# Edge counts kept as running totals and subtracted on reload, and chunk maxima carried in bfloat16 parts, in a graph network

## What is computed

```python
def sage(x, Wl, bl, Wr):                       # twice
    agg = segment_sum(x[src], dst) / max(deg, 1)
    return relu(agg @ Wl + bl + x @ Wr)
# gru: messages = segment_sum(x[src] @ W + b + embed[edge_type], dst); x = gru_cell(messages, x)
# gin, three layers: agg = segment_sum(relu(h[src] + edge_attr_16 @ W), dst); a two-layer MLP follows
def gat(x, ea, Wl, bl, Wr, br, We, att):       # three layers, 4, 4 and 1 heads
    xl, xr = x @ Wl + bl, x @ Wr + br
    m = leaky(xl[src] + xr[dst] + ea @ We)
    s = (m * att).sum(-1)                      # one score per edge and head
    smax = segment_max(s, dst)
    ex = exp(s - smax[dst])
    return segment_sum(xl[src] * ex, dst) / segment_sum(ex, dst)
```

## Time and profile before

| | us |
|---|---|
| median of 3 runs | 11598.76 |
| lowest and highest | 11585.36, 12062.77 |
| the profiled execution | 11593.12 |
| its span, first to last instruction | 11591.3 |
| busy in the span: TensorE, VectorE, ScalarE, GpSimd | 7698.1, 5644.0, 3139.2, 4843.4 |
| counting stage, sage 1, gat stages | 120 to 1506, 1534 to 1764, 6233 to 11550 |

### The profile page before, as it was taken

The page is one execution under the profiler, slowest core; times in us unless marked ns, Lnnn a source line. Parts: engine busy times, 40 slices in busy tenths (PEclk is TensorE's granted clock), DMA queues, the critical chain, the costliest instruction groups (busy, mean ns, idle before and its releaser), DMA issues. The chain is left out here.

```text
span 11591.3 us, 187130 instructions
## 1 busy us (share of the span) xinstructions
PE 7698.1 (66%) x44683; PEld 5505.4 (47%) x44684; DVE 5644.0 (49%) x15775; ACT 3139.2 (27%) x10374; POOL 4843.4 (42%) x5412
## 2 busy tenths in 40 slices
PE   5998888644554444544546777776777776777776
PEld 2444478433343223322334555555555554555554
DVE  6888811222222222222224565666555666555556
ACT  1000130111111111101113444444444444333333
POOL 0011100365554665465653444443444443444442
PEclk9999999766676666666667777777777777777777
DMA  1000076222221111111111222221222221222221
GB/s 35 17 28 39 40 295 233 91 67 66 68 70 50 47 47 47 44 47 46 48 46 46 57 59 57 58 56 52 59 58 57 59 56 49 58 57 58 57 56 45
DMA packets 501818, 732.17 MB, mean 63 GB/s; under 512 B 128746, under 2 KB 406594, under 8 KB 485013
## 3 DMA queue, kind: packets, MB, share of 16 engines
q1 hardware_dynamic: 350484, 414.14, 10.8%
q0 software_dynamic: 150528, 308.58, 10.3%
HBM read 597.78 MB, written 124.32 MB: 62 GB/s over the span
## 5 line engine op out<-in xcount | busy, mean ns | idle before, releaser
L542 POOL DMA_INDIRECT rows_and_onehots<-node_table,idx x4704 | 4560.3, 969 | 2748.4 <-issue 1373.3
L802 PE MATMUL ps<-rows_and_onehots,w 128*128 128x128 f32 x5280 | 1010.7, 353 | 2010.6 <-ACT w L674 1464.1
L802 PEld LDWEIGHTS ps<-rows_and_onehots,w 128*128 128x128 f32 x5280 | 940.9, 260 | 2597.3 <-issue 2564.8
L674 ACT ACTIVATE w<-w 128x512 f32<-128x512 f32 x663 | 417.5, 630 | 3387.8 <-DVE w L1224 2776.9
L951 PE MATMUL ps<-w_L_gnn_We,hr 128*128 128x512 f32 x1344 | 1113.3, 923 | 174.6 <-issue 119.7
L537 POOL COPY idx<-src_g 128x8 int32 (+1 forms) x594 | 115.3, 194 | 2541.4 <-DVE hr L1407 1111.9
L1224 DVE TENSOR_TENSOR w<-rows_and_onehots,ps 128x512 f32<-128x512 f32 x663 | 456.2, 688 | 1272.3 <-issue 689.8
L962 PE MATMUL ps<-hr,rows_and_onehots 128*128 128x132 f32 (+1 forms) x5280 | 955.5, 335 | 116.3 <-DVE hr L1407 87.3
L954 PEld LDWEIGHTS ps<-xrb,w 128*128 128x128 bf16 x8064 | 715.8, 125 | 634.8 <-issue 634.8
L1353 DVE TENSOR_TENSOR w<-rows_and_onehots,ps 128x512 f32<-128x512 f32 x669 | 458.5, 685 | 1042.1 <-remote 817.5
L978 PE MATMUL ps<-ident,scanned 20*128 20x20 f32 (+1 forms) x1332 | 339.1, 330 | 928.9 <-DVE scanned L1359 791.5
(11 more groups left out here) (223 smaller groups left out, 11786.0 us busy)
## 6 DMA issues: line engine op xcount, KB each, us to landing
w<-turned_onehots_bf SPq DMA_DIRECT2D x672, 128.0 KB
rows_and_onehots<-node_table,idx POOLq DMA_INDIRECT x4704
hr<-in_ea SPq DMA_DIRECT2D x672, 64.0 KB
w<-adjacency_turned SPq DMA_DIRECT2D x26, 1600.0 KB, 7.0
adjacency<-rows_and_onehots SPq DMA_DIRECT2D x25, 1600.0 KB, 5.2
w<-adjacency SPq DMA_DIRECT2D x25, 1600.0 KB, 12.0
rows_and_onehots<-adjacency_turned SPq DMA_DIRECT2D x24, 1600.0 KB, 7.7
turned_onehots_bf<-w SPq DMA_DIRECT2D x224, 128.0 KB
```

The lines of the kernel that those rows point to most:

```text
L542: pool.indirect_dma_start(out=G[q][:, (i % CH) * D:(i % CH + 1) * D], out_offset=None, in_=table[:, :], in_offset=bass.IndirectOffsetOnAxi ...
L802: m = pe.matmul(bank(u % 2, P), rows[u][:, c * D:(c + 1) * D], OH[u][:, c * P:(c + 1) * P], start=(c == 0), stop=(c == CH - 1))
```

## The change

The counting stage stores running totals as they are; GpSimd has no part in it any more. Four comparisons for the targets become one on float32. SP's and ScalarE's waits are for each buffer. In sage 1 the totals come back, three buffers of them, and VectorE subtracts the last tile's total from this one's, bank by bank, in place of the last (`tell_apart`, two tiles ahead of the sum), before TensorE transposes; the transposed tiles have two buffers. The types' totals are subtracted once in a short VectorE stage ("type differences").

In gat the values that go to the nodes are split into three bfloat16 parts (`split_seg`, `rest_of_seg`), the matmul takes them with a bfloat16 one-hot `OHB` that ScalarE makes beside `OH`, and VectorE adds the parts straight from PSUM (`join_seg`), which takes the place of ScalarE's copy. VectorE's order changes.

```diff
...
-        by_target = [w1[:, :], w2[:, :]]
-        by_source = [arena[:, 0:NP], arena[:, NP:2 * NP], hr[:, :]]
+        by_target = [w1[:, :], w2[:, :], hr[:, :]]
+        by_source = [arena[:, 0:NP], arena[:, NP:2 * NP]]
+        types_of_tile = hr[:, 0:TILES * (TYPES + 1)]
...
+        OHB = [spare[RING // 2 + i // 2][:, i % 2 * 256:(i % 2 + 1) * 256].bitcast(BF16) for i in range(RING)]
...
-        segrhs = sb("segrhs", [P, CH * 5])
-        segout = [sb(f"segout{i}", [P, CH * 5]) for i in range(2)]
+        segrhs = sb("segrhs", [P, 3 * CH * 5])
+        segout = sb("segout", [P, CH * 5])
...
-                counted = totals[(t + 1) % 2]
-                sp.wait_ge(tile_counted, t + 1)
-                sp.dma_start(adjacency[t * P:(t + 1) * P, :], counted[:, 0:NP]).then_inc(counts_out, 16)
+                counted = totals[t % 2]
+                sp.wait_ge(bank_copied, PARTS * (t + 2))
+                sp.dma_start(adjacency[t * P:(t + 1) * P, :], counted[:, 0:NP]).then_inc(counts_out[t % 2], 16)
                 sp.dma_start(type_counts[:, t * (TYPES + 1):(t + 1) * (TYPES + 1)],
-                             counted[:, NP:COUNTED]).then_inc(counts_out, 16)
+                             counted[:, NP:COUNTED]).then_inc(counts_out[t % 2], 16)
...
-            for t in range(TILES + 1):
-                if t < TILES:
-                    held(sp, blocks_turned, BANKS * (t - 1))
-                    sp.dma_start(by_target[t % 2], adjacency[t * P:(t + 1) * P, :]).then_inc(counts_in[t % 2], 16)
-                if t > 0:
-                    sp.wait_ge(blocks_copied, BANKS * t)
-                    sp.dma_start(adjacency_t[(t - 1) * P:t * P, :], by_source[(t - 1) % 3]).then_inc(turned_stored, 16)
-            sp.wait_ge(turned_stored, 16 * TILES)
+            for i in range(2):
+                sp.wait_ge(counts_out[i], FLUSH * TILES_OF[i])
+            for t in range(-2, TILES):
+                if t + 2 < TILES:
+                    if t >= 1:
+                        sp.wait_ge(blocks_turned, BANKS * (t + 1))
+                    sp.dma_start(by_target[(t + 2) % 3],
+                                 adjacency[(t + 2) * P:(t + 3) * P, :]).then_inc(counts_in[(t + 2) % 3], 16)
+                if t >= 0:
+                    sp.wait_ge(blocks_copied, BANKS * (t + 1))
+                    sp.dma_start(adjacency_t[t * P:(t + 1) * P, :], by_source[t % 2]).then_inc(turned_stored[t % 2], 16)
...
-            begin(pool, "adjacency")
-            link(pool.memset(totals[1], 0.0))
-            for t in range(TILES):
-                old, new = totals[(t + 1) % 2], totals[t % 2]
-                pool.wait_ge(bank_copied, PARTS * (t + 2))
-                pool.tensor_tensor(old, new, old, ALU.subtract).then_inc(tile_counted, 1)
...
-                if t >= 3:
-                    act.wait_ge(turned_stored, 16 * (t - 2))
-                    act.wait_ge(summed_up, t - 2)
+                if t >= 2:
+                    act.wait_ge(turned_stored[t % 2], 16 * (t // 2))
+                    act.wait_ge(summed_up, t - 1)
                 for b in range(BANKS):
                     act.wait_ge(blocks_turned, BANKS * t + b + 1)
-                    act.copy(by_source[t % 3][:, columns_of(b)], ps[:, columns_of(b)]).then_inc(blocks_copied, 1)
+                    act.copy(by_source[t % 2][:, columns_of(b)], ps[:, columns_of(b)]).then_inc(blocks_copied, 1)
...
-                    if on(s + 2):
-                        act.wait_ge(S["seg_max"], s + 3)
-                        act.copy(segout[u % 2][:, 0:CH * (H + 1)], bank(5, CH * (H + 1))).then_inc(S["seg_out"], 1)
...
+                    act.activation(OHB[(u + AHEAD) % RING], far, ACT.Relu, scale=-1.0, bias=1.0)
...
-                pe.wait_ge(counts_in[t % 2], 16 * (t // 2 + 1))
+                if t == 0:
+                    pe.wait_ge(counts_in[0], 16)
                 for b in range(BANKS):
                     if t:
+                        pe.wait_ge(blocks_apart, BANKS * (t - 1) + b + 1)
                         pe.wait_ge(blocks_copied, BANKS * (t - 1) + b + 1)
+                    counted = by_target[max(t - 1, 0) % 3]
                     for j in BLOCKS[b]:
-                        m = pe.transpose(ps[:, j * P:(j + 1) * P], by_target[t % 2][:, j * P:(j + 1) * P], ident[:, :])
+                        m = pe.transpose(ps[:, j * P:(j + 1) * P], counted[:, j * P:(j + 1) * P], ident[:, :])
...
+                seg_parts = segrhs[:, 0:3 * CH * (H + 1)].bitcast(BF16).rearrange("p (k x half) -> p k x half", k=3,
+                                                                                 half=2)[:, :, :, 1]
...
-                        pe.wait_ge(S["seg_rhs"], s + 3)
+                        pe.wait_ge(S["seg_parts"], s * 3 + 9)
                         held(pe, S["seg_out"], s + 2)
                         for c in range(CH):
-                            m = pe.matmul(seg_max[:, c * (H + 1):(c + 1) * (H + 1)],
-                                          OH[(u + 2) % RING][:, c * P:(c + 1) * P],
-                                          segrhs[:, c * (H + 1):(c + 1) * (H + 1)], start=True, stop=True)
+                            m = pe.matmul(seg_max[:, c * 3 * (H + 1):(c + 1) * 3 * (H + 1)],
+                                          OHB[(u + 2) % RING][:, c * P:(c + 1) * P],
+                                          seg_parts[:, :, c * (H + 1):(c + 1) * (H + 1)], start=True, stop=True)
...
-                for c in range(CH):
-                    dve.tensor_scalar(TARGETS[u % 2][:, c * P:(c + 1) * P], local_ids, dloc[:, bass.ds(s * CH + c, 1)], None,
-                                      ALU.is_equal)
+                dve.tensor_tensor(TARGETS[u % 2].rearrange("p (c d) -> p c d", d=P),
+                                  dloc[:, bass.ds(s * CH, CH)][:, :, None].to_broadcast([P, CH, P]),
+                                  iota_d[:, None, :].to_broadcast([P, CH, P]), ALU.is_equal)
...
+            def tell_apart(t):
+                total, last_total = by_target[t % 3], by_target[(t - 1) % 3]
+                dve.wait_ge(counts_in[t % 3], 16 * (t // 3 + 1))
+                if t == 1:
+                    dve.wait_ge(counts_in[0], 16)
+                    dve.wait_ge(blocks_turned, BANKS)
+                for b in range(BANKS):
+                    cs = columns_of(b)
+                    dve.tensor_tensor(last_total[:, cs], total[:, cs], last_total[:, cs],
+                                      ALU.subtract).then_inc(blocks_apart, 1)
             def sums_of(name):
                 stage(name)
                 first = 0 if name not in SUMS else TILES * (1 + SUMS.index(name))
+                if not first:
+                    tell_apart(1)
                 for t in range(TILES):
+                    if not first and t + 2 < TILES:
+                        if t:
+                            dve.wait_ge(blocks_apart, BANKS * (t + 1))
+                        tell_apart(t + 2)
...
+            dve.tensor_copy(types_of_tile[:, 0:T1], type_counts[:, 0:T1])
+            link(dve.tensor_tensor(types_of_tile[:, T1:TILES * T1], type_counts[:, T1:TILES * T1],
+                                   type_counts[:, 0:(TILES - 1) * T1], ALU.subtract))
+            dve.tensor_scalar(rdeg[:, :], types_of_tile.rearrange("p (t k) -> p t k", k=T1)[:, :, TYPES], 1.0,
+                              None, ALU.max).then_inc(turn, 1)
...
+                def join_seg(s, u):
+                    dve.wait_ge(S["seg_max"], s + 1)
+                    dve.tensor_reduce(by_chunk(segout[:, 0:CH * (H + 1)]),
+                                      seg_max.rearrange("p (c k h) -> p c h k", c=CH, k=3), AX.X,
+                                      ALU.add).then_inc(S["seg_out"], 1)
...
+                def split_seg(s, u):
+                    dve.wait_ge(S["seg_parts"], s * 3 + 1)
+                    dve.tensor_tensor(segrhs[:, SR:2 * SR], segrhs[:, 0:SR], high_half(segrhs[:, 0:SR]),
+                                      ALU.subtract).then_inc(S["seg_parts"], 1)
...
+                def rest_of_seg(s, u):
+                    dve.wait_ge(S["seg_parts"], s * 3 + 2)
+                    dve.tensor_tensor(segrhs[:, 2 * SR:3 * SR], segrhs[:, SR:2 * SR], high_half(segrhs[:, SR:2 * SR]),
+                                      ALU.subtract).then_inc(S["seg_parts"], 1)
...
-                closing = [(attend, 3), (chunk_max, 1), (seg_rhs, 2), (new_max, 1), (sum_scores, 3), (split_max, 1),
-                           (take_sums, -1), (rest_of_max, 1), (weigh, 0)]
+                closing = [(join_seg, 1), (seg_rhs, 2), (attend, 3), (split_seg, 2), (chunk_max, 1), (rest_of_seg, 2),
+                           (sum_scores, 3), (new_max, 1), (take_sums, -1), (split_max, 1), (weigh, 0), (rest_of_max, 1)]
...
```

66 lines of the change are left out of this document (37 added, 29 removed).

## The result

The changed kernel took 11441.52 us (median of 4; 11411.97 to 11460.68) beside 11600.62 for the kernel before on the same chip: ratio 0.9865, 95% interval 0.9832 to 0.9897. That is 1.35% faster, under the 2% that the prediction calls a difference, and 380 us above the forecast of 11060. One of the four runs of the kernel before took 12062.77 us, 4% more than the others, and the ratio is formed without it. The profiled execution of the changed kernel took 11411.97 us, its span is 11410.2.

The account below looks back on a forecast made before the run. Counting was taken as bound by TensorE starved during GpSimd's subtractions, sage 1 by TensorE and DMA, gat by TensorE, directly or through late results. 11593.1 minus 165, 5, 0 and 363 gave 11060 us, range 10770 to 11450.

Parts of the forecast that it names:

- Counting: Counting stage: without GpSimd's subtractions, VectorE and TensorE no longer stall at tile ends; 165 us saved, high bound 174.
- The hand-over: After counting: a copy, short subtraction and maximum on VectorE replace GpSimd's last 5.87 us subtraction; 5 us saved.
- Sage 1: Sage 1: VectorE, nearly idle, takes the subtractions; 0 us change, range -5 to +25.
- The lock is something else: Rival, counting: VectorE stalls at tile ends without GpSimd too; 165 us less gain, 11225 us; chance 0.03.
- Gat, the price of the work: Gat: new bfloat16 chunk-maximum matmuls take 0.28 us per step for 1.24; 0.96 us less, 640 us over three stages.
- What of the 0.96 arrives depends on the step: Gat: share of TensorE's saving reaching the time, by clock and gathers; 0.73 us, 0.55 after lower clock, 363 us total.
- the clock case: Rival, gat: idler TensorE's clock falls from 0.73 to 0.65, leaving 92 us gain; 11330 us, up to 11440; chance 0.20.
- The 4.83 us step at the full clock: Gat, full clock without gathers (25%): step is 4.83 us, VectorE's new 5.2 takes over; a loss of 0.35 us.
- VectorE's 0.48 us: Gat: join_seg and two splits add 0.48 us of VectorE work per step, to 5.2 us.
- Bursts of gathers fix VectorE's waits: Rival, gat: VectorE's 3.1 us idle per step lasts as long as GpSimd's gathers; 317 us lost, 11740 us; chance 0.07.
- The clock takes it back: Rival, gat: less work makes TensorE idler, its clock falls to 0.65, 92 us gain remains; 11330 us; chance 0.20.

Follow-up runs that it names:

- more_tensor: The changed kernel with the old four float32 chunk-maximum matmuls put back ahead of the new ones: 11754.20 us, ratio 0.9979 to the kernel before.
- gat_alone: The kernel before with only the gat half of the change, counting and sage as before: 11787.68 us, ratio 0.9996 to the kernel before.
- count_alone: The kernel before with only the counting and sage half of the change, old gat, three semaphores merged: 11630.60 us, ratio 0.9880.
- sets 1 to 3: Follow-up runs, each set on one chip beside the kernel before, which took 11600 to 11794 us on these chips and the result's.
- after_half: The changed kernel with two of each group's four gathers left out in the gat stages: 9754.44 us, ratio 0.8267 to the kernel before.
- sets 4 and 5: Follow-up runs, each set on one chip beside the kernel before, which took 8913 us on these chips.
- changed_again: The changed kernel, nothing altered, run again on a chip where the kernel before took 8913.31 us: 8731.41 us, ratio 0.9794.
- after_none: The changed kernel with no indirect DMA (gathers) in the gat stages: 9705.09 us, ratio 0.8239 to the kernel before.

## Why the prediction was wrong

*Counting: right.* 120.28 to 1332.76 is 1212.5 us, 174 less than the 1386.5 before; I took 165 with 174 as the bound: all that the stage lost above 5.50 us a step, except its slow first step, came back. *The hand-over: right*: from the last count to the first transposition 22.4 us (27.5 before), 5 less. *Sage 1: right*: 213 us from its first transposition to its end, 219 before; I said 0, between 5 less and 25 more, and it is just past the lower bound. The subtractions took 0.69 us each, not 0.61: that row is a mean over six 128x512 additions of 0.66 us and one 128x128 of 0.26. *The lock is something else*: refuted, since the source one-hots, which the change left alone, are never held once GpSimd's subtractions are gone.

*Gat, the price of the work: right.* 647 us less TensorE work for 640; the new matmuls are 178.8 / 666 = 0.27 us per step for 0.28.

*Gat, "What of the 0.96 arrives depends on the step": this step failed.* I had seen late results behind GpSimd's bursts, wrote "So the gat step is a TensorE step, directly or through late results", and took them for TensorE being late, so that a shorter list would make it less late: 0.8 us of 0.96 at the full clock with gathers, 1.2 at the half clock. The three stages, each from its first projection to its last, summed to 5161 us before and 5139 after: 22 us, 0.03 us per step in place of 0.55. In the burst the matmuls are done and their semaphores are late, so less work means a longer wait (262 to 412 us of "remote"); behind the burst VectorE's step decides. "The prediction is wrong if the gat stages don't change in length", I had written, and they didn't. The half clock was read the wrong way round too: in the cycle above it is the clock after a wait of 6.1 us (two scan_back matmuls take 0.61 us at 6416.41 and 0.39 at 6405.37), and no sign that TensorE is the limit. more_tensor puts the worth of a microsecond of TensorE at 0.15; I had taken 0.73 of the 0.96, or 0.55 after the clock's share.

*The range.* 11441.5 lies inside 10770 to 11450, but by luck: only the far end of the clock case reached up there, and that mechanism was refuted.

*The 4.83 us step at the full clock* as TensorE's limit, with VectorE's 5.2 a loss of 0.35: right in sign. Where nothing is late the new gat is 28 to 33 us slower.

*VectorE's 0.48 us* was too much. Its busy time in a stage rose from 1029 to 1063 us, 0.16 per step: small operations start before the one ahead of them ends, 0.09 us apart for durations of 0.16 (VectorE's timeline, changed kernel):

```profile
6401.47 0.16 DVE L1437 TENSOR_TENSOR segrhs<-segrhs 128x20 f32<-128x20 f32 x1
6401.56 0.16 DVE L1344 SCALAR_TENSOR_TENSOR sval<-segout 128x16 f32<-128x16 f32 x1
```

So durations of small operations don't add up; windows do.

*Rivals.* "Bursts of gathers fix VectorE's waits" had the mechanism. Its sign to look for, VectorE idle for 3.1 us per step rather than 2.1, came: (1725 - 1063) / 220 = 3.0, and 3.0 in the last stage. Its price of 317 us was VectorE's 0.48 on every step; with 0.16, on every second step, and TensorE's 0.15 of 0.96 against it, no loss is left. I gave it 0.07. "The clock takes it back" was refuted: 0.74 and 0.74 for 0.73. The Trainium skill's rule ("TensorE: Matmul & The Clock Gate", section "HAM oscillation — how this bites in real kernels") held as far as it goes, for the clock is at 0.74 with the late semaphores and at 0.91 without them, in the same loop; but the clock is what the waits cause, not what ate the saving.

What remains: by the prices above the new gat should save 0.15 x 640 = 96 us and lose half of 3 x 34, 51, so gain 45. Measured were 22 less in the stages of the result, 14 more in those of gat_alone beside count_alone's, and 6 less in the whole time of gat_alone, whose interval allows a gain of at most 22. Each of the two prices carries the changed kernel's interval of 38 us either way, so the difference shows nothing. In the profiled execution gin, which the change doesn't touch, took 27 us longer (3966 before, 3993 after), which accounts for the whole being 181 us and not the 207 of the parts (174 + 5 + 6 + 22).

## What to carry to other kernels

If an engine waits for a result whose record ended long ago, shortening the work in that record may shorten next to nothing (here a microsecond was worth 0.15): ask what the moment of the wait's end coincides with, and take that away in one run (here: leave the gathers out) before making anything faster. In a cycle of a burst and a step, moving the operation that ends the step, or putting waits into the burst, gave 165 to 415 us where 647 us less work gave none, on the chips where the semaphores are late; on the others there was nothing to gain by it. A subtraction of totals moved to an engine idle in the next stage gave all that its waits promised.

## What the runs showed of the hardware

On the chips of the result and of sets 1 to 3, TensorE's semaphore increments reached the other engines late while GpSimd issued indirect DMAs: in the changed kernel's first gat stage 40% of those that can be matched, up to 8.6 us, and half of the late ones 0.7 to 1.6 us after the end of the latest gather. VectorE's did not come late in the cycle shown. With pairs of gathers only (after_half) 6 of 1247 were late, without gathers none. On the chips of sets 4 and 5 none was late, with the same kernel and the same 0.96 to 0.97 us per gather; the whole kernel took 24% less (8913 for 11794 us). Each gather counts its semaphore up in sixteen increments (the Trainium skill, "DMA: Bandwidth & Descriptors", section "Why a DMA increments its semaphore by 16 and not by 1"), 64 for a group. The first kind's trace has 16 records of changes per group in the first gat stage, changed_again's 60. The increments are missing from the record only, for GpSimd's wait for all 64 ended. VectorE's own increments are missing in the same way (3157 of 4195 recorded in the changed kernel's first gat stage, 4087 in changed_again's, all in after_none's). Many increments on the way to the semaphores at once would fit this, and so would the recording holding them up. Every execution here was recorded, so no run tells the two apart, and the cause stays open.

VectorE's comparison of 128x512 on float32 with two broadcast inputs takes 693 ns, as its plain tensor_tensor operations of that size do (662 to 695 ns in the same trace). One GpSimd subtraction of 128x3210 float32 (5.87 us) held VectorE's comparisons for its whole length: four took 6.41 us, and the next four, at 1032.45, took 0.73.
